# The first expert's weights get a place outside the attention's buffers and are split mostly in the body before the last; sums, sixth tile and last norm stand later

## The chip, the cores and the metric

One core of one Trainium2 chip. The metric is the device time of one launch in microseconds (us); lower is better. The kernel before was timed three times: median 1436.99 us, from 1432.22 to 1437.5.

## The reference, cut to what matters

32 batches of 112 tokens, width 256. First a gated cross-attention over 375 context rows and the 112 normed tokens themselves, 8 heads of 64; then a layer of 8 experts of inner width 1024, of which each token takes the best two.

```python
x = x + tanh(g_xattn) * attention(ctx_1024, layernorm(x), mask, ...)      # softmax over 487 keys
h = layernorm(x)
bids = sigmoid(h @ conf_w.T + conf_b) * wealth                            # 8 bids per token
top_bids, chosen = top_k(bids, 2); weight = softmax(top_bids)
expert(h) = (silu(h @ gate_w.T) * (h @ up_w.T)) @ down_w.T
x = x + tanh(g_ffn) * sum over the chosen of weight * expert(h)
```

## The kernel before, in words

Every matrix product is done in halves: each operand is scaled by a power of two and split into a high and a low f16 part (names ending in `_hi`, made on ACT, and `_lo`, made on DVE), and TensorE (PE) multiplies three of the four pairs.

**Attention.** A loop over the batches, written out as 32 bodies b = 0 to 31 (B = 32, so B - 1 is body 31, the last). Each body has eight slots h, one per head, and every engine has its own program for a slot. In slot h of body b PE computes scores (`sims`, two heads at once in even slots), transposes of the probabilities (`probs_T`), products with the values (`values`), one or two projections for the next batch (`piece`, into the two PSUM tiles `fP`), and what is left of batch b - 1 (`heads_T`, `out_proj`, `norm2_T`). ACT does exponentials (L769), high halves of probabilities (L776) and projections (L762); DVE does the masked maximum (`masked_max`, tile `ms`, L1036), the low halves (L1042, L1026), the residual of batch b - 1 (`residual`, L1067, which frees the store of `x1`) and the routing arithmetic. Each engine takes its own program strictly in order; semaphores tie them.

**Experts.** Tokens are written to `routed_rows` by expert (GpSimd's indirect DMAs, `scatter`), and a second loop runs over NT = 63 tiles of 128 rows: transpose of the tile (`tile_T`), `gate_up` for the two halves i = 0, 1 of the inner width (into `gP`, `uP`), `silu` on ACT, `gated` on DVE, transpose (`act_T`), and `down` into `yP`, weighted by `weigh` and added to `out` by a DMA (`add_tile`). In step t PE takes `act_T(t - 1, 1)`, `tile_T(t + 1)`, `gate_up(t, 0)`, `gate_up(t, 1)`, `down(t - 1)`. Only the first AHEAD = 5 tiles, of the fullest expert, can be read before all tokens are scattered; tile 5, the sixth, is the first that needs every scatter to have landed.

**An expert's weights.** They come as f32 into `raw` in six pieces of 128 x 1024 and are split into `W2`. The stages, by name: `expert_squares` (ACT, L854, sums of squares of a piece), `expert_sums` (PE, L1655, adds them over the partitions), `expert_bound` (DVE, L1245), `expert_pow` (GpSimd, L522), `expert_scale` (DVE, L1251 to L1258), and per piece `expert_hi` (ACT, L864) and `expert_lo` (DVE, L1263). For the first expert to be used, number 0, all this happens during the last attention bodies: which slot gets which piece is written by hand in `SPLIT_SQ`, `SPLIT_HI` and `SPLIT_LO`; which expert it is, is worked out on DVE in the twelve steps of `ORDER_AT` (the last of them writes `first_i`, L1225), and then SyncE loads it (`load_raw(0)`, L394). For later experts p the same is spread over five tiles: squares after tiles with t % 5 = 0, 1, 2, sums, bound and scale at t % 5 = 3, the split at 3, 4 and 0. From p = 2 on `expert_sums(p)` stands between the two halves of `gate_up` and `expert_bound(p)` ahead of `gated(t, 1)`.

**Memory.** The expert loop's buffers share the memory of the attention's. `W2` has five places of 24 KB per partition: four that are used by PE and one in which experts 4 to 7 are split before they go to DRAM (`split_experts`). The attention's buffers reach up to about 136 KB. The first place lies over `kT0`, `v0` and `qT0`, which body 30 still reads; the wait on `s_pv` in `expert_hi` keeps the first split behind that body.

**The end of the attention.** SyncE's program (the queue of its DMAs) after the last body's loads is: store of `x1` of batch 30, which waits for `residual(30)` in slot 7 of body 31; eight writes of padding rows (`routed_rows<-padrows`, L423); the six pieces of expert 1 (`load_raw(1)`); and only then the store of `x1` of batch 31. GpSimd waits for that last store before it goes into the expert loop, whose first steps are the eight scatters of the last four batches (`scatter_last`) among two `add_tile`, and then the load of tile 5 (`load_tile`, tile `xt`).

Of the kernel before, what the change touches and what calls it, by code (L numbers as in the profile page):

```python
# [14 lines left out]
P = 128  # L15
# [67 lines left out]
SPLIT_SQ = {(B - 3, 7): (0,), (B - 2, 1): (1,), (B - 2, 2): (2,), (B - 2, 5): (3,), (B - 2, 6): (4,), (B - 2, 7): (5,)}  # L83
SPLIT_HI = {(B - 1, 4): (0,), (B - 1, 5): (1,), (B - 1, 6): (2,), (B - 1, 7): (3,)}
SPLIT_LO = {(B - 1, 5): (0,), (B - 1, 6): (1,), (B - 1, 7): (2,)}
ORDER_AT = {(B - 4, 0): (0, 1), (B - 4, 6): (2, 3, 4), (B - 4, 7): (5, 6, 7), (B - 3, 0): (8, 9, 10, 11)}
# [4 lines left out]
def build(nc, x, ctxt, mask, scal, lnw, wqkv, wout, confw, confbw, wffn, out):  # L91
# [4 lines left out]
    with ctx:  # L96
# [153 lines left out]
        W2 = sb("W2", [P, SLOTS + 1, 2, WCOL], F16, pb)  # L250
# [4 lines left out]
        ysb = [sb(f"ysb{i}", [P, D], F32, pb) for i in range(2)]  # L255
        ppb = ExitStack()
# [78 lines left out]
        def in_place(p):  # L335

            return min(p, SLOTS)
# [12 lines left out]
        def _(sp):  # L350
# [61 lines left out]
            def load_place(n):  # L412

                step_ = WCOL // RELOADS
                for c in range(RELOADS):
                    sp.dma_start(W2[:, n % SLOTS, :, c * step_:(c + 1) * step_],
                                 wsp[n - SLOTS, :, :, c * step_:(c + 1) * step_]).then_inc(s_there, 16)
# [23 lines left out]
        def _(pool):  # L441
# [82 lines left out]
            def put_pieces(p, some):  # L524
# [3 lines left out]
                pool.dma_start(wsp[p - SLOTS, :, :, cols], W2[:, SLOTS, :, cols]).then_inc(s_wput, 16)  # L528
# [60 lines left out]
            def body(b, g, q):  # L589
# [7 lines left out]
                if holds(b, 0, B - 4):  # L597
                    rstd(b + 3)
                if b == B - 1:
                    expert_pow(0)  # L600
# [99 lines left out]
        def _(act):  # L700
# [155 lines left out]
            def expert_hi(p, c):  # L856

                if c == 0:
                    act.wait_ge(s_esc, p + 1)
                    if p == 0:  # L860
                        act.wait_ge(s_pv, H * (B - 1))
# [49 lines left out]
            def step(t, k):  # L911
# [17 lines left out]
                if t == AHEAD - 1:  # L929
                    tile_hi(t + 1, 1 - q)  # L930
                if t < NT:
                    if 0 not in TURNED:
                        act_hi(t, q, 0)
                    silu(t, 1, place)
                    if 0 in TURNED:
# [8 lines left out]
            def tail():  # L944

                probs_hi(B - 1, H - 2)
                expert_hi(0, 4)
# [3 lines left out]
                expert_hi(0, 5)  # L951
# [15 lines left out]
        def _(dve):  # L967
# [301 lines left out]
            def body(b, g, q):  # L1269
# [4 lines left out]
                for h in range(H):  # L1274
# [48 lines left out]
                    if (b, h) == (B - 1, 2):  # L1323
                        expert_bound(0, fP[0])
                    if (b, h) == (B - 1, 3):
# [97 lines left out]
            def step(t, k, place, last_place):  # L1423
# [13 lines left out]
                if t == AHEAD - 1:  # L1437
                    tile_lo(t + 1, 1 - q)
# [4 lines left out]
                if p < E and j == 3 and p > 1:  # L1443
                    expert_bound(p, bP)
                if t < NT:
                    gated(t, 1, place)
                    if 0 in TURNED:
# [5 lines left out]
                if p < E and j == 3 and p > 1:  # L1453
                    expert_scale(p)
# [18 lines left out]
            def tail():  # L1473
# [3 lines left out]
                expert_lo(0, 3)  # L1477
# [5 lines left out]
                expert_lo(0, 4)  # L1483
# [389 lines left out]
```

## Time and profile before

| | |
|---|---|
| time, median of three | 1436.99 us |
| the profiled execution | 1435.85 us, span 1434.3 us |
| PE busy | 1351.1 us, 94% |
| DVE busy | 1023.5 us, 71% |
| ACT busy | 934.8 us, 65% |
| GpSimd busy | 488.2 us, 34% |
| mean granted clock of PE | 0.989 of full |

The times in the rows further down are microseconds from the start of the span. The attention's bodies take up about the first 850 us, some 25 us each; the expert loop the rest, about 8.6 us a tile.

### The profile page before, as it was taken

Reading aid. Unit: us, or ns where it says so; the run is one execution under the profiler, and the core shown is the slowest. Engines: PE = TensorE matmul, PEld = TensorE weight load, DVE = VectorE, ACT = ScalarE, POOL = GpSimd, SP = SyncE. Lnnn points to the kernel's source line nnn. Section 1 sums busy time; section 2 is a strip of 40 time slices with the busy share of each in tenths; the row PEclk is TensorE's granted clock in tenths of the full one; section 3 lists DMA queues with packets and bytes.
Section 4 is the critical chain, followed back from the end, with each engine's and each line's share of the span. In section 5 each row is a group of like instructions: output and inputs, shape, how many; then the busy total and the mean of one; then the engine's idle time right before and its main releaser. Section 6 shows DMA issues by size and latency. Waiting matters only on the chain.

```text
span 1434.3 us, 41525 instructions
## 1 busy us (share of the span) xinstructions
PE 1351.1 (94%) x13880; PEld 969.2 (68%) x13880; DVE 1023.5 (71%) x2528; ACT 934.8 (65%) x1932; POOL 488.2 (34%) x659
## 2 busy tenths in 40 slices
PE   2999999999999999999999979999999999999996
PEld 1466666666666666666665657688878778887784
DVE  4688888888888888888888776566556654444442
ACT  5687878787787878878787765566656663333331
POOL 4423322433433334334333143433344333222221
PEclk9999999999999999999999979999999999999998
DMA  4010101111111111111112146433376753112461
GB/s 119 27 42 26 42 23 29 52 40 49 34 53 30 41 46 39 49 33 53 31 33 96 41 129 196 107 98 93 98 211 178 228 152 94 31 31 35 120 203 16
DMA packets 56913, 109.26 MB, mean 76 GB/s; under 512 B 10832, under 2 KB 34768, under 8 KB 56720
## 3 DMA queue, kind: packets, MB, share of 16 engines
q0 software_dynamic: 23712, 55.71, 15.2%
q1 hardware_dynamic: 32160, 49.86, 11.2%
q8 instruction: 126, 2.06, 0.6%
q10 hardware_dynamic: 848, 1.07, 0.3%
q14 instruction: 67, 0.55, 0.1%
HBM read 69.16 MB, written 37.45 MB: 74 GB/s over the span
## 4 chain that ended last, share of the span: by engine, by line
PE 70%; DVE 10%; ACT 6%; issue 6%; DMA 5%; SPq 1%; POOL 1%; POOLq 0%; DVEq 0%; ACTq 0%
PE fP L1542 19%; PE yP L1542 10%; PE uP L1542 10%; PE gP L1542 10%; PE simP L1590 5%; PE ptP L1600 4%; PE tP L1542 3%; PE oP L1542 3%; DVE ms L1036 3%; DVE pT L1042 2%; DMA out<-ysb,xt 2%; PE aP L1773 2%; DVE ao L1054 1%; ACT z L732 1%; PE fP L1558 1%
## 5 line engine op out<-in xcount | busy, mean ns | idle before, releaser
L1542 PE MATMUL fP<-zTs,ws 128*128 128x112 f16 (+1 forms) x1536 | 220.3, 294 | 8.7 <-DVE zTs L1378 5.3
L1542 PE MATMUL fP<-ws,zTs 128*128 128x512 f16 x768 | 186.8, 379 | 0.5 <-DVE kT L1026 0.2
L1036 DVE CUSTOM_DVE_ANT_0 ms<-simP,madd,sim_undo 112x488 f32<-112x488 f32 x256 | 183.9, 720 | 3.3 <-PE simP L1590 1.3
L769 ACT ACTIVATE pr<-ms,nmax 112x488 f32<-112x488 f32 x256 | 179.0, 699 | 3.3 <-DVE nmax L1036 0.5
L1042 DVE SCALAR_TENSOR_TENSOR pT<-ptP,pT 122x448 f16<-122x448 f32 x256 | 157.8, 616 | 28.0 <-ACT pT L776 27.3
L1542 PEld LDWEIGHTS fP<-zTs,ws 128*128 128x128 f16 x1536 | 109.8, 99 | 99.7 <-issue 34.9
L1542 PE MATMUL yP<-W,aT 128*128 (+1 forms) x1512 | 175.4, 273 | 1.8 <-DVE aT L1414 1.8
L1542 PEld LDWEIGHTS yP<-W,aT 128*128 128x128 f16 x1512 | 147.6, 98 | 32.8 <-issue 2.5
L1408 DVE SCALAR_TENSOR_TENSOR act_h<-uP,consts,sg 128x512 f32<-128x512 f32 x126 | 94.5, 750 | 103.1 <-ACT sg L899 102.7
L776 ACT ACTIVATE pT<-ptP 122x448 f16<-122x448 f32 x256 | 137.8, 538 | 40.8 <-PE ptP L1600 39.7
L899 ACT ACTIVATE sg<-gP,consts 128x512 f32<-128x512 f32 x126 | 86.5, 686 | 114.6 <-PE uP L1542 114.4
L641 POOL DMA_INDIRECT out<-ysb,xt x63 | 105.2, 1670 | 157.4 <-DVE ysb L1421 143.8
L1542 PE MATMUL oP<-v,pT 122*128 122x64 f16 x3072 | 133.6, 194 | 14.0 <-DVE pT L1042 9.1
L1600 PE MATMUL ptP<-ident,pr 112*122 112x112 f32 x1024 | 142.0, 261 | 0.4 <-DVE filled L1148 0.4
L499 POOL TENSOR_TENSOR zTs<-zT,zTs 128x1200 f16<-128x1200 f32 x31 | 76.5, 2469 | 193.1 <-ACT zTs L750 193.1
L1542 PEld LDWEIGHTS oP<-v,pT 122*128 122x128 f16 x3072 | 121.0, 98 | 26.6 <-DVE pT L1042 26.5
L1600 PEld LDWEIGHTS ptP<-ident,pr 112*122 112x122 f32 x1024 | 114.2, 139 | 25.6 <-issue 0.8
L1542 PEld LDWEIGHTS fP<-ws,zTs 128*128 128x128 f16 x768 | 67.9, 98 | 82.1 <-issue 14.4
L1590 PE MATMUL simP<-kT,qT 64*128 64x488 f16 x768 | 102.7, 372 | 13.3 <-DVE nmax L1036 12.4
L1026 DVE SCALAR_TENSOR_TENSOR kT<-fP,kT 128x488 f16<-128x488 f32 x128 | 84.9, 664 | 37.2 <-ACT kT L762 37.2
L762 ACT ACTIVATE kT<-fP 128x488 f16<-128x488 f32 x128 | 73.8, 576 | 51.4 <-PE fP L1542 51.3
L1026 DVE SCALAR_TENSOR_TENSOR v<-fP,v 122x512 f16<-122x512 f32 x128 | 88.3, 690 | 26.5 <-ACT v L762 26.0
(233 smaller groups left out, 2496.2 us busy)
## 6 DMA issues: line engine op xcount, KB each, us to landing
raw<-wffn POOLq DMA_DIRECT2D x36, 512.0 KB, 6.9
split_experts<-W POOLq DMA_DIRECT2D x12, 1024.0 KB, 10.0
W<-split_experts SPq DMA_DIRECT2D x16, 768.0 KB, 7.9
xc<-ctxt SPq DMA_DIRECT2D x32, 375.0 KB
xt<-routed_rows POOLq DMA_DIRECT2D x63, 129.0 KB, 2.4
raw<-wffn SPq DMA_DIRECT2D x12, 512.0 KB, 9.5
routed_rows<-padrows SPq DMA_DIRECT2D x8, 645.0 KB, 7.9
xl<-x SPq DMA_DIRECT2D x32, 112.0 KB
```

The lines of the kernel that those rows point to most:

```text
L499: nc.gpsimd.tensor_tensor(zTs[p][:, 1, :, :], zT[:, :, :], zTs[p][:, 0, :, :], ALU.subtract).then_inc(s_zsplit, 1)
L641: pool.indirect_dma_start(out[:, :], bass.IndirectOffsetOnAxis(ap=xt[k][:, D:D + 1].bitcast(I32), axis=0), ysb[t % 2][:, :], None, compute ...
L769: nc.scalar.activation(pr[h % 2][:, :], ms[h % 2][:, :], ACT.Exp, bias=nmax[p][:, h:h + 1], scale=-1.0, accum_out=rsum[p][:, h:h + 1]).the ...
L776: nc.scalar.activation(pT[h % 2][:, 0, :, 0:S], ptP[h % 2][0:KR, :, 0:S], ACT.Copy, scale=P_TOP).then_inc(s_pthi, 1)
L899: nc.scalar.activation(sg[i][:, :], gP[i][:, :], ACT.Silu, scale=constant(place, 0)).then_inc(s_silu, 1)
L1026: nc.vector.scalar_tensor_tensor(out=o, in0=i, scalar=1.0 / TOP, in1=hi, op0=ALU.mult, op1=ALU.subtract).then_inc(s_plo, 1)
L1036: nc.vector.tensor_tensor_reduce(out=ms[h % 2][:, :], in0=simP[h % 2][0:S, 0:NK], in1=madd[p][:, :], scale=sim_undo[0:S, 0:1], scalar=3.0e ...
L1042: nc.vector.scalar_tensor_tensor(out=pT[h % 2][:, 1, :, 0:S], in0=ptP[h % 2][0:KR, :, 0:S], scalar=P_TOP, in1=pT[h % 2][:, 0, :, 0:S], op0 ...
L1408: nc.vector.scalar_tensor_tensor(out=act_h[i][:, :], in0=uP[i][:, :], scalar=constant(place, 2), in1=sg[i][:, :], op0=ALU.mult, op1=ALU.mu ...
L1542: last = nc.tensor.matmul(o, lhs(k, a), rhs(k, c), start=n == 0, stop=n == len(todo) - 1)
L1590: last = nc.tensor.matmul(simP[i][:, 0:NK], qT[p][r, a, h // 2, :], kT[p][r, c, h // 2, :], start=t == 0, stop=t == len(PARTS) - 1)
L1600: last = nc.tensor.transpose(ptP[h % 2][0:KR, c, 0:S], pr[h % 2][:, c * KR:(c + 1) * KR], ident[0:S, 0:S])
```

## The change

The order in which `W2` and the buffers around it are laid out changes: `W2` now stands last, and expert 0 uses its fifth place, above all the attention's buffers. The places are renumbered for this (`in_place`, `in_slot`), and the wait on `s_pv` falls away. The twelve ordering steps move up within body 28; the six pieces of squares go from bodies 29 and 30 to 28 and 29; sums, bound, power and scale from body 31 to body 30, with a wait on PE before `fP[0]` is written again; the split of the six pieces from slots 4 to 7 of body 31 and the tail to slots 3 to 7 of body 30 and 0, 1 of body 31. In the expert loop `tile_T(5)` and its halves go behind `gate_up(4, 1)` and `gated(4, 1)`; `expert_sums(p)` for p from 2 goes behind `gate_up(t, 1)`, and `expert_bound(p)` next to `expert_scale(p)` behind `gated(t, 1)`. In PE's tail `norm2_T(31)` goes behind the whole of `gate_up(0, 1)`.

```diff
-SPLIT_SQ = {(B - 3, 7): (0,), (B - 2, 1): (1,), (B - 2, 2): (2,), (B - 2, 5): (3,), (B - 2, 6): (4,), (B - 2, 7): (5,)}
-SPLIT_HI = {(B - 1, 4): (0,), (B - 1, 5): (1,), (B - 1, 6): (2,), (B - 1, 7): (3,)}
-SPLIT_LO = {(B - 1, 5): (0,), (B - 1, 6): (1,), (B - 1, 7): (2,)}
-ORDER_AT = {(B - 4, 0): (0, 1), (B - 4, 6): (2, 3, 4), (B - 4, 7): (5, 6, 7), (B - 3, 0): (8, 9, 10, 11)}
+SPLIT_SQ = {(B - 4, 6): (0,), (B - 4, 7): (1,), (B - 3, 0): (2,), (B - 3, 3): (3,), (B - 3, 5): (4,), (B - 3, 7): (5,)}
+SPLIT_HI = {(B - 2, 3): (0,), (B - 2, 4): (1,), (B - 2, 5): (2,), (B - 2, 6): (3,), (B - 2, 7): (4,), (B - 1, 0): (5,)}
+SPLIT_LO = {(B - 2, 4): (0,), (B - 2, 5): (1,), (B - 2, 6): (2,), (B - 2, 7): (3,), (B - 1, 0): (4,), (B - 1, 1): (5,)}
+ORDER_AT = {(B - 4, 0): (0, 1), (B - 4, 1): (2, 3), (B - 4, 3): (4, 5, 6, 7), (B - 4, 4): (8, 9, 10, 11)}
...
         def in_place(p):
-            return min(p, SLOTS)
+            return (min(p, SLOTS) + SLOTS) % (SLOTS + 1)
+        def in_slot(n):
+            return (n % SLOTS + SLOTS) % (SLOTS + 1)
...
+                if b == B - 2:
+                    expert_pow(0)
                 if b == B - 1:
-                    expert_pow(0)
                     first_rows(0, 2)
...
-                    if p == 0:
-                        act.wait_ge(s_pv, H * (B - 1))
...
-                if t == AHEAD - 1:
-                    tile_hi(t + 1, 1 - q)
                 if t < NT:
...
                     silu(t, 1, place)
+                    if t == AHEAD - 1:
+                        tile_hi(t + 1, 1 - q)
...
-                    if (b, h) == (B - 1, 2):
+                    if (b, h) == (B - 2, 1):
                         expert_bound(0, fP[0])
-                    if (b, h) == (B - 1, 3):
+                    if (b, h) == (B - 2, 3):
                         expert_scale(0)
...
-                if p < E and j == 3 and p > 1:
-                    expert_bound(p, bP)
                 if t < NT:
                     gated(t, 1, place)
+                    if t == AHEAD - 1:
+                        tile_lo(t + 1, 1 - q)
...
                 if p < E and j == 3 and p > 1:
+                    expert_bound(p, bP)
                     expert_scale(p)
...
                     if holds(b, 0, B - 2):
+                        if (b, h) == (B - 2, 2):
+                            pe.wait_ge(s_ech, 1)
...
-                    if (b, h) == (B - 1, 1):
-                        pe.wait_ge(s_plo, seq(B - 2, NPIECE))
+                    if (b, h) == (B - 2, 1):
+                        pe.wait_ge(s_plo, seq(B - 2, PQ + 1) + 1)
                         expert_sums(0, fP[0])
...
-                gate_up(0, 0, 1, 0, (0,))
+                gate_up(0, 0, 1, byte_of(0))
                 norm2_T(B - 1, (B - 1) % 4)
-                gate_up(0, 0, 1, 0, (1,))
...
-                if t == AHEAD - 1:
-                    tile_T(t + 1, (t + 1) % XT_BUFS)
-                if SPAN < t and t // SPAN + 1 < E and t % SPAN == 3:
-                    expert_sums(t // SPAN + 1, bP)
...
                     gate_up(t, q, 1, byte)
+                if t == AHEAD - 1:
+                    tile_T(t + 1, (t + 1) % XT_BUFS)
+                if SPAN < t and t // SPAN + 1 < E and t % SPAN == 3:
+                    expert_sums(t // SPAN + 1, bP)
```

## Rows read from the trace of the kernel before

**Rows 1.** Busy us (x instructions) of PE, PEld, DVE, ACT, POOL, PE's clock, DMA, by stretch.
```profile
773.73:799.40 25.67, 24.39 (x254) 16.18 (x255) 21.09 (x57) 18.69 (x43) 6.23 (x6) 1.00 0.46 157
799.40:824.30 24.90, 23.93 (x247) 15.28 (x247) 19.18 (x50) 20.38 (x48) 4.11 (x6) 1.00 0.07 21
824.30:847.20 22.90, 17.35 (x202) 12.41 (x202) 20.10 (x62) 17.67 (x40) 6.50 (x9) 0.83 0.16 44
...
1200.00:1300.00 100.00, 100.00 (x1062) 81.16 (x1061) 43.24 (x70) 33.08 (x58) 25.94 (x24) 1.00 0.19 35
```
**Rows 2.** Timeline of PE around tile 5: start us, us, instruction, idle before it.
```profile
900.40 0.44 PE L1737 MATMUL xP<-ident,xt 128*128 128x128 f32 x2 [2.85 <-DMA xt<-routed_rows]
900.67 2.38 PE L1542 MATMUL gP<-W,xT 128*128 128x512 f16 x6
...
904.95 2.79 PE L1542 MATMUL yP<-W,aT 128*128 128x256 f16 x24
...
908.22 1.50 PE L1542 MATMUL gP<-xT,W 128*128 128x128 f16 x24
```
**Rows 3.** The chain that ended last, from the last store to tile 5.
```profile
868.72 11.23 DMA out<-x
...
897.91 2.44 DMA xt<-routed_rows
```
**Rows 4.** Timeline of SyncE's DMA queue: expert 0, a store, padding, expert 1.
```profile
779.24 3.28 SPq L394 DMA_DIRECT2D raw<-wffn  x6
...
847.21 0.33 SPq L375 DMA_DIRECT2D out<-x  x1
848.32 12.92 SPq L423 DMA_DIRECT2D routed_rows<-padrows  x8
862.58 6.01 SPq L394 DMA_DIRECT2D raw<-wffn  x6
```
**Rows 5.** Instructions on tile raw, 740 to 825 us: its six loads, from issue.
```profile
DMA to landing us min/median/max: 3.9/6.2/8.5
```
**Rows 6.** Instructions of lines L864, L1263, L854: duration ns min/median/max.
```profile
L864 ACT ACTIVATE W<-raw,escale x48: 1132/1137/1158, 838.2 to 1182.0; 128x1024 f16<-128x1024 f32 x48
L1263 DVE SCALAR_TENSOR_TENSOR W<-raw,escale,W x48: 1273/1276/1285, 840.7 to 1184.7; 128x1024 f16<-128x1024 f32 x48
L854 ACT ACTIVATE junk<-raw x48: 1041/1056/1074, 800.2 to 1159.7; 128x1024 bf16<-128x1024 f32 x48
```
**Rows 7.** Timeline of DVE in body 30, slots 5 and 7.
```profile
818.82 0.62 DVE L1042 SCALAR_TENSOR_TENSOR pT<-ptP,pT 122x448 f16<-122x448 f32 x1 [0.80 <-ACT pT L776]
...
823.43 0.72 DVE L1036 CUSTOM_DVE_ANT_0 ms<-simP,madd,sim_undo 112x488 f32<-112x488 f32 x1
```
**Rows 8.** Timeline of DVE in body 31: scale, the third split, residual of batch 30.
```profile
835.15 0.17 DVE L1251 TENSOR_SCALAR ebits<-epow 128x3 int32<-128x3 int32 x1 [0.18 <-POOL epow L522]
...
836.56 0.73 DVE L1036 CUSTOM_DVE_ANT_0 ms<-simP,madd,sim_undo 112x488 f32<-112x488 f32 x1 [0.21 <-DVE consts L1258]
...
845.46 1.27 DVE L1263 SCALAR_TENSOR_TENSOR W<-raw,escale,W 128x1024 f16<-128x1024 f32 x1
846.65 0.48 DVE L1067 SCALAR_TENSOR_TENSOR x<-tP,gates,xres 112x256 f32<-112x256 f32 x1
```
**Rows 9.** PE's waits from 900 us on: waited for, us in total, times, longest.
```profile
PE bP L1655 <- ACT junk L854: 3.2, 3, 1.4
```
**Rows 10.** Timeline of PE at the tile in which expert 5's sums stand.
```profile
1070.15 0.39 PE L1655 MATMUL bP<-esq,ones 128*128 128x6 f32 x2 [1.08 <-ACT junk L854]
...
1072.98 2.78 PE L1542 MATMUL yP<-W,aT 128*128 x24
...
1081.66 2.78 PE L1542 MATMUL yP<-W,aT 128*128 x24
```
**Rows 11.** Timeline of DVE at the same tile: low half of its activations.
```profile
1079.46 0.69 DVE L1414 TENSOR_TENSOR aT<-aP,aT 128x512 f16<-128x512 f32 x1
```
**Rows 12.** Timeline of PE in the tail: the last norm's transposes.
```profile
863.10 0.41 PE L1629 MATMUL tP<-ident,z 112*128 112x112 f32 x2 [1.98 <-DVE z L1081]
```

More of the change, by code:

```diff
@@ L249, in build @@
         junk = sb("junk", [P, PCOL], BF16, pb)
-        W2 = sb("W2", [P, SLOTS + 1, 2, WCOL], F16, pb)
         xT = [sb(f"xT{i}", [P, 2, KD, P], F16, pb) for i in range(2)]
@@ L255, in build @@
         ysb = [sb(f"ysb{i}", [P, D], F32, pb) for i in range(2)]
+        W2 = sb("W2", [P, SLOTS + 1, 2, WCOL], F16, pb)
         ppb = ExitStack()
@@ L415, in load_place @@
                 for c in range(RELOADS):
-                    sp.dma_start(W2[:, n % SLOTS, :, c * step_:(c + 1) * step_],
+                    sp.dma_start(W2[:, in_slot(n), :, c * step_:(c + 1) * step_],
                                  wsp[n - SLOTS, :, :, c * step_:(c + 1) * step_]).then_inc(s_there, 16)
@@ L527, in put_pieces @@
                 pool.wait_ge(s_wlo, p * PIECES + some[-1] + 1)
-                pool.dma_start(wsp[p - SLOTS, :, :, cols], W2[:, SLOTS, :, cols]).then_inc(s_wput, 16)
+                pool.dma_start(wsp[p - SLOTS, :, :, cols], W2[:, in_place(SLOTS), :, cols]).then_inc(s_wput, 16)
             def next_raw(p, c):
@@ L946, in tail @@
                 probs_hi(B - 1, H - 2)
-                expert_hi(0, 4)
                 tile_hi(0, 0)
@@ L950, in tail @@
                 norm2_out(B - 2)
-                expert_hi(0, 5)
                 heads_out_hi(B - 1)
@@ L1436, in step @@
                     gated(t, 0, place)
-                if t == AHEAD - 1:
-                    tile_lo(t + 1, 1 - q)
                 if t < NT and 0 not in TURNED:
@@ L1476, in tail @@
                 norm2(B - 2, (B - 2) % 4)
-                expert_lo(0, 3)
                 tile_lo(0, 0)
@@ L1482, in tail @@
                 logits(B - 2, (B - 2) % 4)
-                expert_lo(0, 4)
                 heads_out_lo(B - 1)
-                expert_lo(0, 5)
                 tile_lo(1, 1)
@@ L1707, in tail @@
                 pe.wait_ge(s_wlo, 4)
-                gate_up(0, 0, 0, 0, (0,))
+                gate_up(0, 0, 0, byte_of(0), (0,))
                 out_proj(B - 1)
-                gate_up(0, 0, 0, 0, (1,))
-                gate_up(0, 0, 1, 0, (0,))
+                gate_up(0, 0, 0, byte_of(0), (1,))
+                gate_up(0, 0, 1, byte_of(0))
                 norm2_T(B - 1, (B - 1) % 4)
-                gate_up(0, 0, 1, 0, (1,))
                 confidences(B - 1)
@@ L1746, in byte_of @@
             def byte_of(place):
-                return place % SLOTS * (2 * WCOL * 2)
+                return in_slot(place) * (2 * WCOL * 2)
             def gate_up(t, q, i, slot_, some=(0, 1)):
@@ L1801, in step @@
                     gate_up(t, q, 0, byte)
-                if t == AHEAD - 1:
-                    tile_T(t + 1, (t + 1) % XT_BUFS)
-                if SPAN < t and t // SPAN + 1 < E and t % SPAN == 3:
-                    expert_sums(t // SPAN + 1, bP)
                 if t == 1:
@@ L1832, in _ @@
             weights_there(0)
-            byte, last_byte = 0, 0
+            byte = last_byte = byte_of(0)
             for t in range(1, NT + 1):
```

## The prediction

> **What bounds the kernel now.** I read the busy times by stretch first. In the expert loop PE has no free time at all [rows 1], so there only PE's own work and its waits count. In the attention's last three bodies it is otherwise: PE is busy for 24.39 of 25.67 us in body 29 and 23.93 of 24.90 in body 30, but only for 17.35 of 22.90 in body 31, at a mean clock of 0.83, while DVE is busy for 20.10 there [rows 1]. So body 31 is bound by DVE and ACT, in which the splitting of expert 0 stands, and bodies 29 and 30 by PE, with DVE and ACT at three quarters to four fifths.
>
> Then PE's timeline in the first tiles. It stands still for 2.85 us at 900.40 for the rows of tile 5 [rows 2], the longest wait of the expert loop. I followed that wait back through the chain of waits: load of tile 5, scatters, GpSimd's wait for the last store of x1, which took 11.23 us from its issue at 868.72 [rows 3]. In SyncE's queue that store stands behind eight padding writes and six pieces of expert 1, issued from 848.32 to 868.6 without a gap, and these behind the store of batch 30 at 847.21 [rows 4], which waits for DVE's residual(30) at 846.65 [rows 8]. This is the clock of the hand-over: **tile 5 arrives 53 us after residual(30)** (900.40 less 847.2), whatever PE does in between. PE's position ahead of tile 5 is worth nothing as long as it gets there first.
>
> Last, PE's waits in the rest of the loop: three times it waits in expert_sums for ACT's squares, 3.2 us in all [rows 9], for experts 5, 6 and 7.
>
> **Part 1: the sixth tile.** Before, tile_T(5) stood ahead of gate_up(4, 1). From the arrival at 900.40 PE had the transposes, gate_up(4, 1), down(3) at 904.95, act_T and a transpose, and began gate_up(5, 0) at 908.22: 7.82 us [rows 2]. After, gate_up(4, 1) runs in the time of the wait. What is left from the arrival on: transposes 0.27 (900.40 to 900.67), and what ran from 904.95 to 908.22, 3.27; 3.54 us, if the clock is full. It was not: gate_up(4, 1) took 4.28 us from 900.67 to 904.95 [rows 2], where the same half and expert 5's sums take 2.83 at full clock, 1070.15 to 1072.98 [rows 10], so 2.6 without the sums; 1.7 us were lost to the half clock (1.2 in place of 2.4 GHz) that the wait brought. Will PE still wait? It now reaches tile_T(5) 2.6 us later in its own work, but the tail gets shorter for it by about as much or more (part 3), so the wait stays near 2.8 us and I take the 1.7 us as lost again: 3.54 + 1.7 = 5.2, gain 7.8 - 5.2 = **2.6 us**. Other end: with no fall of the clock, 4.3. Not less than 2.6 unless the low halves that follow are late: they are hidden by down(3), 2.6 us (2.79 by its row, the pipeline included). What is late next is expert_scale(1), which waits for GpSimd's power; it sits on DVE, and its splits lie under gate_up(5).
>
> The Trainium skill, "TensorE: Matmul & The Clock Gate", section "HAM oscillation", says that a wait for a DMA puts TensorE back to half rate, and that the loss is half of the throttled time. The rows agree here: 4.28 us for 2.6 of work. By that rule the 1.7 us come back whenever PE still waits at tile 5 as long as before; if the sixth tile's move ends the wait, the gain would be 4.3 and not 2.6.
>
> **Part 2: the split, in what it moves residual(30).** One high half takes 1.14 us on ACT, one low half 1.28 on DVE (1.20 from start to start in a row), one square 1.06 and its read-out some 0.15 [rows 6].
>
> *Bodies 28 and 29.* Order of the loads: expert 0's six pieces were issued at 779.24 to 782.5 and landed 3.9 to 8.5 us after issue [rows 4, 5]; the first square was at 800.2 [rows 6]. The order is now known some five slots of 3.1 us (25 / 8) earlier, and the first square stands two slots behind it, 6 us: enough for a first piece at 1 + 3.9 us, with one us to spare, and each next one comes a slot or more later. No wait charged. ACT gets two squares in body 28 and four in 29: 18.69 + 4 x 1.2 = 23.5 of 25.67 us [rows 1], so there is room, but a square in slot 0 of body 29 stands ahead of zT and kT, which free fP for PE. The twelve ordering steps only change places. I charge **0.5 us** (0, all hidden, to 1.5, one and a half squares exposed).
>
> *Body 30.* ACT: five squares out, five high halves in: even. DVE: bound 0.35, scale 1.4 (835.15 to 836.56 [rows 8]), four low halves 4.8: 19.18 + 6.5 = 25.7 us on DVE in a body of 24.90 [rows 1]. DVE becomes the bound of body 30. If every gap were filled the body would grow by 0.8; if none, by 6.5. Most of its gaps are waits for ACT (0.80 at 818.82 is one [rows 7]). Laid out slot by slot with these durations: slot 3 takes the scale with a net 0, slots 4 and 5 each a low half in the gap behind them, but from residual(29) on nothing is left to fill; the last masked maximum of body 30, at 823.43 [rows 7], slides by 2.5 us and the first of body 31 by **3.5**. GpSimd's power is queued ahead of rstd1(29), which waits longer anyway.
>
> *Body 31.* Low halves 4 and 5 in slots 0 and 1 fall into waits for ACT and PE, 0.4 more. Bound and scale leave: -1.6 by slot 4. Three low halves (and four high ones) leave between 836.56 and 846.65 [rows 8], 3 x 1.2 = 3.6, of which the chain scores, exponential, transpose, out_proj gives back 2.6. Residual(30) then is at +3.5 + 0.4 - 1.6 - 2.6 = -0.3, with body 29 at **+0.2 us, that is 0**. With the ends of body 30 (0.8 and 6.5) and of bodies 28 and 29 it is -3 to +4. So the work is moved out of one DVE-bound body into another that becomes so, and tile 5 arrives when it did.
>
> **Part 3: the tail.** Without low halves 3 to 5 PE comes out of the tail earlier against residual(30), by 2 to 3 us, and norm2_T(31), which made PE wait 1.98 us [rows 12], now stands behind 1.3 us more of gate_up. All this is ahead of tile 5, and PE only waits longer there: **0**. It would count in full (some 4 us) only if tile 5 were no longer waited for.
>
> **Part 4: sums later.** 3.2 us of waits [rows 9] end, because gate_up(t, 1), 2.6 us, covers the longest, 1.4. But expert_bound now stands behind gated(t, 1), and DVE then waits for GpSimd's power (0.9 us) ahead of the scale: some 1.2 us more on DVE ahead of weigh(t - 1), two low halves and act_lo(t, 1), six times. At expert 5 act_lo(t, 1) runs from 1079.46 to 1080.15 and down(t) at 1081.66 [rows 10, 11]. PE earlier by 1.1 asks for it at 1080.6, and DVE, without the 0.35 of the bound ahead of gated but with 1.2 behind, ends at about 1080.7: a wait of 0.1. At expert 6, with 1.4, some 0.3. Gain 3.2 - 0.5 = **2.7 us**. Ends: 3.9, if the stretched matmul ahead of each wait counts as well (0.2 each); 0, if the later scale costs PE half a us in each of six tiles.
>
> **Sum.** 2.6 + 0 + 0 + 2.7 = 5.3 us. The profiled execution had 1435.85 us, so 1430.5; it lies 1.1 us under the median of the three, so against the median it is 1431.7. I say **1431 us**.
>
> **The rivals.**
> A, *the hand-over moves up* (faster by more than 0.5%, 7.2 us, about what a measurement of this kernel can tell from no change). DVE's gaps in body 30 take the low halves, residual(30) comes 3 us earlier, and PE's wait at tile 5 ends with the clock held: 4.3 + 3 + 3 = 10.3, 1426 us. For it: DVE has 5.7 us free in body 30 and needs 6.5 [rows 1]. Against it: its gaps come where it waits for ACT, which is busy for 20.38 of 24.90. Chance 0.33.
> B, *body 30 falls behind* (slower side). Each low half there delays the maximum, that the exponential, that the next low half; nothing is hidden, body 30 grows by 6.5, squares cost 1.5, PE's idle time ahead of the ranks in body 31 puts its clock at half for another 3 us, 1.5 lost. Residual(30) is then 4 + 1.5 late or more, and gains of parts 1 and 4 are eaten from 5.3 on: 1435 to 1440, 1437 for the case. To be slower by over 0.5% it takes 12.5 us. For it: PE's maximum, exponential and transpose form one loop. Chance 0.15, of which 0.05 past the bound.
> C, *the scale is the new wait*. Part 4 gives nothing, as at experts 2 to 7 down(t) waits for act_lo(t, 1): 1435.85 - 2.6 = 1433. Against it: act_lo stands 1.5 us ahead of down at expert 5. Chance 0.12.
> D, *tile 5 isn't set by the last store*, and only PE's own order counts; then the tail counts too: 5.3 + 4, 1427. Against it: GpSimd starts its first scatter right as the store lands. Chance 0.05, and on A's side.
>
> **Chances.** My case has 0.35. Its own range is 1428 to 1434. Faster by over 0.5%: A, D, 0.38 less what of A stays under 7.2 us, 0.04, and 0.02 from the edge of my case: 0.36. Slower: 0.05 from B and 0.04 for a mean of stalls that I have not seen: 0.09. The rest, 0.55, is no difference that can be told. The range for 8 in 10 takes in A at 1425 and most of B at 1437.
>
> **What would show it.** Sums of expert 0 in body 30, and bodies 30 and 31 at about 27.5 and 20 us; store of batch 30 at 847 within 3 us; padding and expert 1 behind it at the same pace; tile 5's transpose at about 900 behind gate_up(4, 1), with a wait of some 2 to 4 us and the clock at half in down(3); no waits for L854 in expert_sums, and short ones of yP for DVE's aT instead. I am wrong if residual(30) moves by more than 3 us either way, or if PE no longer waits at tile 5.

## The result, and the profile after

The changed kernel took 1442.93 us in the median of six runs (1440.84 to 1444.42), the kernel before 1435.49 beside it. The ratio is 1.0045, 95% interval 1.0032 to 1.0059: by it the changed kernel is some 6.5 us slower, where I had forecast 5.3 us faster. The profiled execution had 1444.42 us, span 1442.5.

The stretches that answer to [rows 1] (columns as there), bodies 29, 30 and 31 up to the store of batch 30:

```profile
773.87:801.40 27.53, 24.90 (x255) 16.24 (x255) 20.16 (x50) 23.76 (x55) 6.90 (x7) 1.00 0.30 101
801.40:828.69 27.29, 24.22 (x249) 15.55 (x249) 23.80 (x62) 20.98 (x45) 5.69 (x6) 1.00 0.06 19
828.69:851.86 23.17, 17.79 (x197) 13.14 (x198) 18.68 (x53) 14.36 (x34) 4.79 (x8) 0.78 0.14 37
```

Body 29 is 1.9 us longer, body 30 2.4, and body 31, from which DVE lost 1.4 and ACT 3.3 us of work, is no shorter. Below is the queue of SyncE's DMAs, which answers to [rows 4]:

```profile
851.86 0.33 SPq L379 DMA_DIRECT2D out<-x  x1
852.98 13.88 SPq L427 DMA_DIRECT2D routed_rows<-padrows  x8
868.22 5.78 SPq L398 DMA_DIRECT2D raw<-wffn  x6
874.12 0.45 SPq L379 DMA_DIRECT2D out<-x  x1
```

The store of batch 30 goes out 4.65 us later than before, the last store 5.4 later. PE's timeline around tile 5, which answers to [rows 2], and down(5) at the end of the next tile:

```profile
904.18 1.46 PE L1539 MATMUL gP<-W,xT 128*128 128x512 f16 x6
...
906.77 0.40 PE L1735 MATMUL xP<-ident,xt 128*128 128x128 f32 x2
907.70 2.78 PE L1539 MATMUL yP<-W,aT 128*128 128x256 f16 x24 [0.52 <-DVE aT L1415]
...
910.97 1.50 PE L1539 MATMUL gP<-xT,W 128*128 128x128 f16 x24
...
916.67 0.50 PE L1539 MATMUL yP<-W,aT 128*128 128x256 f16 x3 [0.27 <-DVE aT L1415]
```

The wait for tile 5 is all but gone (what is left of it is 0.3 us of a weight load, L1735) and the clock holds: gate_up(4, 1) takes 2.59 us (904.18 to 906.77) in place of 4.28. The step that holds the move, from one act_T to the next, took 9.28 us in place of 13.33. The start of step 1 (its act_T) was 4.75 us later than before (874.63, was 869.88), that of step 5 2.7 us (910.31, was 907.57), and that of step 62 8.4 (1417.00, was 1408.64). So the loop behind tile 5 lost 5.6 us more, although the waits of [rows 9] are gone. These are the three longest rows of PE's list of waits from 860 us on (in all, times, longest):

```profile
PE yP L1539 <- DVE aT L1415: 2.7, 5, 1.5
PE tP L1626 <- DVE z L1082: 1.0, 1, 1.0
PE uP L1539 <- issue: 0.9, 3, 0.4
```

From 907 to 1420 us all of PE's waits come to 2.4 us, and before to 5.3. So no new wait pays for the 5.6 us: most of them lie in matmuls that got slower. This is tile 10 before (PE, and the gated that its act_T waits for on DVE):

```profile
950.31 0.75 DVE L1408 SCALAR_TENSOR_TENSOR act_h<-uP,consts,sg 128x512 f32<-128x512 f32 x1 [0.33 <-ACT sg L899]
...
952.01 0.60 PE L1773 MATMUL aP<-ident,act_h 128*128 128x128 f32 x4
...
952.66 1.50 PE L1542 MATMUL gP<-xT,W 128*128 128x128 f16 x24
954.00 1.56 PE L1542 MATMUL uP<-xT,W 128*128 128x128 f16 x24
955.46 1.46 PE L1542 MATMUL gP<-W,xT 128*128 x6
```

and after:

```profile
954.41 0.75 DVE L1409 SCALAR_TENSOR_TENSOR act_h<-uP,consts,sg 128x512 f32<-128x512 f32 x1
...
955.44 0.60 PE L1771 MATMUL aP<-ident,act_h 128*128 128x128 f32 x4
...
956.10 1.69 PE L1539 MATMUL gP<-xT,W 128*128 128x128 f16 x24
957.75 1.96 PE L1539 MATMUL uP<-xT,W 128*128 128x128 f16 x24
959.70 1.46 PE L1539 MATMUL gP<-W,xT 128*128 x6
```

The same 48 products of gate_up(10, 0) take 3.60 us, 956.10 to 959.70, in place of 2.80. No wait stands at them, the clock is full. What differs is how late gated(9, 1) ended ahead of the act_T in front of them: 0.28 us (955.16 to 955.44) in place of 0.95. I call this the **lead** below. In the changed kernel gate_up(t, 0) takes 3.4 us or more in tiles 6, 10, 15, 20, 24, 25, 30, 34, 35 and 61, always behind a lead of at most 0.28 us but for the last; before it was so in 6, 20, 32 (leads of 0.24 and less) and 61. In tiles 6, 24 and 30 PE also stood 0.2 to 0.3 us ahead of act_T, in the others before 61 not at all.

The lead doesn't explain all of the 5.6 us. In the two traces the steps 5 to 35 lost 3.1 us and the steps 36 to 61 lost 2.5, and from 36 to 60 every lead is 0.94 or 0.95 as before. Of the 2.5 us 1.5 are spread over the steps 36 to 59, some 0.06 in each (e1_arith says from what), and 1.0 stands in steps 60 and 61, where PE now waits 0.54 us for the last expert's weights (`W<-split_experts`).

Nor does a short lead cost anything in every tile. This is tile 3 before:

```profile
885.52 0.63 PE L1773 MATMUL aP<-ident,act_h 128*128 128x128 f32 x4 [0.62 <-DVE act_h L1408]
...
886.20 1.50 PE L1542 MATMUL gP<-xT,W 128*128 128x128 f16 x24
...
888.88 1.46 PE L1542 MATMUL gP<-W,xT 128*128 128x512 f16 x6
```

PE even waits for gated(2, 1), which ended 0.26 us ahead of act_T, and the 48 products take 2.68 us (886.20 to 888.88). It is so in tiles 2 (leads from 0.65 up) and 3 of every kernel that keeps act_T ahead of gate_up(t, 0), with one exception: tile 3 of the changed kernel, 3.75 us with two stalls of PE in it. What sets the tiles below 5 apart in the kernel is that their expert is number 0, so the address of its weights is a constant of the program; from tile 5 on it is read from a table and stands in a register. No run here swaps the two.

### The profile page after: what moved, and what is told of

Its sections match the earlier page's. It is cut to its first block, busy times and chain, and to the rows that moved or that the text cites. A ratio compares the mean times of both kernels' runs of the same rounds, so it can differ in the third digit from the quotient of the medians.

```text
span 1442.5 us, 41531 instructions
## 1 busy us (share of the span) xinstructions
PE 1360.9 (94%) x13880; PEld 976.4 (68%) x13880; DVE 1022.9 (71%) x2528; ACT 933.5 (65%) x1932; POOL 487.2 (34%) x659
## 4 chain that ended last, share of the span: by engine, by line
PE 71%; DVE 10%; ACT 7%; issue 6%; DMA 4%; POOL 1%; SPq 1%; DVEq 0%; POOLq 0%; ACTq 0%; another core or an unknown queue 0%
PE fP L1539 18%; PE uP L1539 10%; PE gP L1539 10%; PE yP L1539 10%; PE simP L1587 5%; PE ptP L1597 4%; PE oP L1539 3%; PE tP L1539 3%; DVE ms L1037 2%; DVE pT L1043 2%; PE aP L1771 2%; DMA W<-split_experts 1%; DVE ao L1055 1%; ACT z L737 1%; PE fP L1555 1%
```

## The experiments

Each run was timed in five rounds against the kernel before on the same chip; a ratio is to that kernel, with its 95% interval, and 0.1% is 1.4 us.

**e1_arith: the longer place arithmetic alone.**
```diff
-                return place % SLOTS * (2 * WCOL * 2)
+                return (place % SLOTS + SLOTS + 1) % (SLOTS + 1) * (2 * WCOL * 2)
```


> The kernel before with one edit: the line that turns an expert's place into a byte offset takes one addition and one more modulo, as in the changed kernel, with the same value as before. Layout, schedule and order of work stay. Theory P (place arithmetic in TensorE's queue): after the changed kernel's tile 5 the loop lost 5.7 us against before although its sums won 3.3, and 48 products of some gate_up(t, 0) start 75 ns apart in place of 56; if the longer arithmetic is what leaves the queue without a lead, this run is slower than before by 4 to 9 us, with more tiles of some 9.4 us. Theory M (the new layout of the memory slows the products): no change, within 1 us. Theory S (the loop is slow only because the schedule ahead of it differs): no change.

1.0000 (0.9990 to 1.0011). Theory P is out as the main cause: at most 1.6 us. A small part of it stays: the 24 steps 36 to 59, in which nothing is split, took 208.21 us here and 207.91 to 208.29 in the eight traces with this arithmetic (the changed kernel, e1, e2, e4, e8, e9, e15, e16), against 206.80 to 207.24 in the five with the old one and no other edit there (before, e5, e6, e7, e12). That is some 1.1 us, 0.05 a tile, at the same lead of 0.95.

**e2_layout: the new layout alone**, with that arithmetic and without the wait on s_pv.


> The kernel before with only the new layout: W2 last, places renumbered with the longer arithmetic, no wait on s_pv. Schedule of the split, sixth tile, sums and last norm as before. Theory M: slower by 4 to 9 us, all of it in the expert loop, and more than e1_arith. Theory P: the same time as e1_arith within 1 us. Theory S: within 1 us of before.

1.0015 (1.0004 to 1.0027). The expert loop from step 5 to 62 took 501.08 us against 501.07: theory M is out. In the trace the 2 us lie ahead of the loop: 0.4 came by PE's wait for the ranks in body 31, and 1.4 more by residual(30); e7_bound_early has those 1.4 too, with no edit there, so they can be chance (last section). The steps 36 to 59 took 1.1 us more than before, as in e1_arith. What else the ratio's 2.2 us hold has no mechanism here.

**e3_cheap: places counted downwards.**
```diff
-            return (n % SLOTS + SLOTS) % (SLOTS + 1)
+            return SLOTS - n % SLOTS
```


> The changed kernel with the places counted downwards (expert n in place 4 - n % 4, the fifth used in place 0), so that one modulo and one subtraction do where the changed kernel has two modulos and an addition. Expert 0 still lies above the attention's buffers. Theory P: faster than the changed kernel by 2 to 6 us, 1437 to 1441. Theories M and S: 1443, as the changed kernel.

1.0083 (1.0070 to 1.0096), 5.5 us slower than the changed kernel: a miss. It was not cheaper. Its page counts 41647 instructions, the changed kernel's 41531: 116 more, which would be two for each of the 58 tiles whose expert is read from a table (e1_arith counts 41525, as before). In tiles 36 to 53 gate_up(t, 0) takes 2.91 to 3.07 us against 2.72 to 2.88, at the same lead.

**e4_oldsplit: the changed kernel with the old schedule** of orders, squares, sums and split.


> The changed kernel with the split's old schedule: orders, squares, sums, bound, power, scale and the six splits stand where they stood before; layout, longer arithmetic, sixth tile, later sums and last norm are as changed. If the schedule costs what residual(30) and the tail show (4.65 and 3.9 us later), this run is faster than the changed kernel by 3.5 to 5 us, 1438 to 1439.5, with bodies 30 and 31 and residual(30) as before. Rival (the loss all arises in the expert loop, since PE would have waited for tile 5 anyway): 1442 to 1443.

1.0016 (1.0002 to 1.0029). Against the changed kernel's 1.0045 that is 4.2 us: the schedule costs what I expected here, and the rival is out. Residual(30) is back at 846.10, where the kernel before had 846.65.

**e5_sums: part 4 alone.**


> The kernel before with part 4 alone: expert_sums(p) behind gate_up(t, 1) and expert_bound(p) next to expert_scale(p). My forecast of the part: 2.7 us faster than before. Theory L, formed on the traces so far: the later scale pushes ACT's high halves and with them gated(t - 1, 1) to within 0.3 us of the transpose act_T that waits for it (0.95 us otherwise), and the gate_up(t, 0) behind such a late arrival takes 3.5 to 3.6 us in place of 2.8. By L the waits for L854 go (3.2 us) but gate_up(t, 0) of tiles 10, 15, 25, 30, 35 (and one or two more) is 0.8 us longer: between 1 us faster and 3 us slower than before.

1.0020 (1.0007 to 1.0032): 2.9 us slower. The waits of [rows 9] are gone, and gate_up(t, 0) of tiles 10, 15, 25, 29, 30 and 35 took 3.56, 3.46, 3.41, 3.52, 3.72 and 3.63 us, at leads of 0.10 to 0.25: 4.7 us more than before in these six. The profiled execution was the fastest of the twelve (1437.17), and its loop from step 5 to 62 took 501.09 us against 501.07; so this trace shows the gain eaten, and not the 2.9 us on top.

**e6_sixth: part 1 alone.**


> The kernel before with part 1 alone: tile 5's transpose and halves behind gate_up(4, 1). My forecast: 2.6 us faster, 4.3 if the clock stays full. By the changed kernel's trace, in which the fifth step took 9.28 us in place of 13.33, it is 4 us, unless tile 5's rows come later than TensorE; then each us of that wait is lost again. So 3 to 4 us faster, and 1 us of that lost again if act_lo(4, 1) is only just ready for down(4).

0.9990 (0.9976 to 1.0004), 1.4 us faster, less than expected but with 3 us inside the interval. In its trace step 4 takes 9.58 us in place of 13.33, and step 5 0.8 us more (9.38), with a wait of down(4) for act_lo.

**e7_bound_early: the sums later, the bound where it was.**


> The kernel before with only the move of expert_sums(p) behind gate_up(t, 1); expert_bound(p) keeps its place ahead of gated(t, 1). Then GpSimd's power and the scale are not later by more than the sums themselves, and what DVE waits for in expert_bound lies under the silu. Theory L: the waits for the squares go and no gate_up(t, 0) is stretched in exchange: 2 to 3.5 us faster than before, and faster than e5_sums by 2 to 5 us. Rival (gate_up is stretched for another reason than the late gated): the same time as e5_sums.

0.9994 (0.9982 to 1.0006): no change against before, but 3.7 us faster than e5_sums. Tiles 10, 15, 25 and 35 are back at 2.89, 2.77, 2.71 and 2.85 us. Why it still gains nothing is seen at experts 5 to 7: ACT's squares are late as before (they wait for raw), act_lo of the same tile comes 0.14 us ahead of down in place of 1.68, and gate_up of tiles 24, 29 and 34 takes 3.52, 3.19 and 3.68 us. The waits moved.

**e8_after_bound: the same in the changed kernel**
```diff
                 if p < E and j == 3 and p > 1:
-                    expert_bound(p, bP)
                     expert_scale(p)
...
+                if p < E and j == 3 and p > 1:
+                    expert_bound(p, bP)
                 if t < NT:
                     gated(t, 1, place)
```


> The changed kernel with one edit: expert_bound(p) stands ahead of gated(t, 1) again, the sums stay behind gate_up(t, 1). Theory L: the stretched gate_up(t, 0) of tiles 10, 15, 25, 30, 35 go back to 2.8 us, 3 to 5 us faster than the changed kernel, 1438 to 1440. Rival (stretched for another reason, such as the new place of the weights): no change, 1443.

1.0015 (1.0003 to 1.0027), 4.3 us faster than the changed kernel. Theory L holds, the rival is out. Tiles 10, 15 and 35 are back at 2.89, 2.81 and 2.86 us; 25 (3.35, lead 0.35) and 30 (3.21, lead 0.68) only in part.

**e9_squares: the changed kernel with only orders and squares early.**


> The changed kernel with only the orders and squares early (in bodies 28 and 29); sums, bound, power, scale and the split stand where they stood before. It stands between e4_oldsplit (both old) and the changed kernel (both new), which are 4.2 us apart. From the changed trace: body 29 is 1.9 us longer than before, body 30 2.4 and residual(30) 4.65 later. If the squares in bodies 28 and 29 are what makes body 29 longer, this run is about 1.9 us slower than e4_oldsplit, 1441, with body 30 starting at 801.4 and as long as before (24.9); the rest, 2.4, is the low halves in body 30. Rival: all 4.2 us come from body 30, then 1439.

1.0032 (1.0020 to 1.0045), 2.3 us slower than e4_oldsplit. Body 30 started at 801.3 and was 24.6 us long. So of the schedule's 4.2 us, 2.3 are the squares and 1.9 the rest, each give or take some 1.8.

**e10_late: DVE late on purpose, PE never waiting.**
```diff
+                late = 0 if i == 0 else 256 if 38 <= t < 45 else 512 if 47 <= t < 54 else 0
+                if late:
+                    nc.vector.scalar_tensor_tensor(out=junk[:, 0:late], in0=uP[i][:, 0:late], ...)
                 nc.vector.scalar_tensor_tensor(out=act_h[i][:, :], in0=uP[i][:, :], ...
```


> The kernel before with work added on DVE alone, in tiles without any split: ahead of gated(t, 1) the same operation once more into a scratch buffer, 256 columns wide (some 0.4 us) in tiles 38 to 44 and 512 wide (some 0.7 us) in tiles 47 to 53. The output stays the reference's. TensorE never has to wait for DVE there: act_T follows the end of gated 0.95 us later, so both leave it 0.2 us and more. Plain reading of the waits (what doesn't end a wait costs nothing): same time as before. Theory L: gate_up(t + 1, 0) is longer by 0.3 to 0.5 us in seven tiles and by 0.7 to 0.8 in the other seven, 7 to 9 us slower than before, about 1444.

1.0055 (1.0038 to 1.0072): 7.9 us slower. This is DVE and PE in one tile of the first group:

```profile
1217.45 0.48 DVE L1410 SCALAR_TENSOR_TENSOR junk<-uP,consts,sg 128x256 bf16<-128x256 f32 x1 [0.29 <-ACT sg L899]
1217.85 0.74 DVE L1412 SCALAR_TENSOR_TENSOR act_h<-uP,consts,sg 128x512 f32<-128x512 f32 x1
```
```profile
1228.83 1.50 PE L1546 MATMUL gP<-xT,W 128*128 128x128 f16 x24
1230.17 1.90 PE L1546 MATMUL uP<-xT,W 128*128 128x128 f16 x24
1232.03 1.46 PE L1546 MATMUL gP<-W,xT 128*128 x6
```

The second fence is the following tile: the first 24 products run at 56 ns (1.34 / 24), the next 24 at 78 (1.86 / 24). The seven tiles behind the small dose (lead 0.56 in place of 0.95) were 0.40 us longer each, the seven behind the large one (0.29) 0.66 each: 7.4 us in all. No wait of PE stands in the trace from 1195 to 1360 us. The added operation can't slow the products by running beside them, since it ends ahead of act_T. So for the tiles from 5 on theory L is shown by intervention; why a short lead costs is not.

**e11_turn: the kernel before with act_T(t - 1, 1) behind gate_up(t, 0)**, ACT and DVE in the same order.
```diff
-                act_T(t - 1, 1)
...
                 if 1 < t < NT:
                     gate_up(t, q, 0, byte)
+                    act_T(t - 1, 1)
```


> The kernel before with act_T(t - 1, 1) behind gate_up(t, 0) in each tile, and ACT and DVE in the same order; every product as before. The wait for gated(t - 1, 1), which stood right ahead of the short products of gate_up(t, 0), is then long fulfilled when TensorE comes to it. Theory L: gate_up(t, 0) takes its shortest time, 2.68 us, in all tiles: 0.1 us won in some 55 tiles and 0.8 in three or four, 5 to 9 us faster than before, unless down(t - 1) now waits for act_lo (0.8 us of slack by the rows), which would cost 0.3 us a tile, and 10 us slower in the worst case. Rival (gate_up is stretched by its own reads of the weights): no gain, or slower.

0.9973 (0.9961 to 0.9986): 3.9 us faster. Two tiles in a row:

```profile
1090.82 0.38 PE L1743 MATMUL xP<-ident,xt 128*128 128x128 f32 x2
1091.04 1.50 PE L1548 MATMUL gP<-xT,W 128*128 128x128 f16 x24
1092.38 1.50 PE L1548 MATMUL uP<-xT,W 128*128 128x128 f16 x24
1093.72 0.61 PE L1779 MATMUL aP<-ident,act_h 128*128 128x128 f32 x4
...
1099.37 0.38 PE L1743 MATMUL xP<-ident,xt 128*128 128x128 f32 x2
```

In all but six of the tiles 5 to 61 the 48 products take 2.67 to 2.69 us, and most tiles are 8.55 us long. The exceptions are tiles 7, 10, 20, 32, 35 and 61, with 2.82, 2.71, 3.17, 3.50, 2.75 and 3.90 us. The gain is under 5 to 9 us because step 31 (10.70) waits 1.16 us for DVE's act_lo ahead of down, which also stretches tile 32, and because PE waits in step 60 (11.12) for the last expert's weights on their way back from DRAM:

```profile
1395.61 0.44 PE L1743 MATMUL xP<-ident,xt 128*128 128x128 f32 x2 [1.14 <-DMA W<-split_experts]
1395.88 1.95 PE L1548 MATMUL gP<-xT,W 128*128 128x128 f16 x24
```

**e12_best: parts 1, 3's last norm and the later sums, with the bound early**, on the kernel before.


> The kernel before with the sixth tile's move, the last norm's move and the later sums with the bound kept ahead of gated(t, 1); layout and schedule of the split as before. Measured singly: -1.2 us for the sixth tile, 0 for the sums with the early bound. If these add: 1 to 3 us faster than before, 1433 to 1435. Rival (the last norm's move brings something by itself, which no run has shown alone): 3 to 4 us faster.

0.9975 (0.9956 to 0.9994), 3.6 us faster. The interval doesn't tell the forecast from the rival.

**e13_both: e11_turn and e12_best together.**


> e12_best and e11_turn together: the kernel before with the sixth tile and last norm later, sums later with the bound early, and act_T(t - 1, 1) behind gate_up(t, 0). Singly they are 0.25% and 0.27% faster than before. If they add in full: 7.5 us, 1428. By theory L they add in part only: e12_best still has some seven stretched gate_up (tiles 20, 24, 29, 30, 32, 34, 61), which e11_turn removes too, but e11_turn has two waits of some 1 us for DVE's act_lo at tiles 28 and 31: 5 to 8 us, 1427 to 1431.

0.9947 (0.9931 to 0.9964): 7.6 us faster than before, the best of all. Singly they gave 3.9 and 3.6: they add, as far as the intervals tell.

**e14_after_turn: the changed kernel, turned.**


> The changed kernel with the same order as e11_turn. If the part of its loss that lies in the expert loop is all the lead of TensorE's queue ahead of gate_up(t, 0), the turned loop takes every step in 8.55 us whatever DVE's lateness, and this run comes out at e11_turn plus what the schedule costs (4.2 us) less what the sixth tile brings (1 to 3): 1433 to 1436, 7 to 10 us faster than the changed kernel. Rival (part 4 costs by something else too): 1437 or more.

1.0007 (0.9994 to 1.0019), 5.5 us faster than the changed kernel, less than expected, and the rival is partly right: steps 9, 19, 24, 29 and 34 still take 9.2 to 9.6 us, because with the late scale act_lo is only 0.13 to 0.27 us ahead of down.

**e15_spaced: the squares later and in other slots.**
```diff
+SPLIT_SQ = {(B - 3, 3): (0,), (B - 3, 4): (1,), (B - 3, 5): (2,), (B - 3, 6): (3,), (B - 3, 7): (4,), (B - 2, 0): (5,)}
```


> The changed kernel with the six squares in slots 3 to 7 of body 29 and slot 0 of body 30 in place of slots 6 and 7 of body 28 and 0, 3, 5, 7 of body 29. In the changed trace three squares run on ACT between 773.5 and 779.9, where ACT has no gap, and zT is 2.5 us later; body 29 is 1.9 us longer. If it is where they stand that costs: body 29 grows by less than 1 us and this run is 1 to 2 us faster than the changed kernel. Rival (ACT's sum over body 29 decides): the same 1443, or slower, since five squares stand in body 29 in place of four.

1.0029 (1.0020 to 1.0037), 2.3 us faster than the changed kernel. Bodies 29, 30 and 31:

```profile
773.90:799.10 25.20, 24.49 (x256) 16.06 (x257) 20.28 (x50) 22.35 (x52) 6.86 (x7) 1.00 0.31 109
799.10:827.30 28.20, 24.39 (x250) 15.58 (x252) 23.87 (x62) 22.03 (x48) 5.71 (x6) 1.00 0.06 18
827.30:850.12 22.82, 19.72 (x184) 14.82 (x184) 18.34 (x51) 14.01 (x33) 4.29 (x6) 0.63 0.12 30
```

Body 29 with five squares is shorter than with four. The place decides, not the sum; body 30 took 0.9 us of it back.

**e16_low31: all six low halves in body 31.**
```diff
+SPLIT_LO = {(B - 1, 0): (0,), (B - 1, 1): (1,), (B - 1, 2): (2,), (B - 1, 3): (3,), (B - 1, 4): (4,), (B - 1, 5): (5,)}
```


> The changed kernel with all six low halves in slots 0 to 5 of body 31; high halves, scale and squares as changed. My forecast was that low halves only move between one DVE-bound body and another: then body 30 is back at some 25 us, body 31 longer by as much, and the time is that of the changed kernel within 1.5 us. Rival 1 (low halves are dearer in body 30, since each delays the loop of maximum and exponential): 1 to 3 us faster than the changed kernel. Rival 2 (body 31, which the last chain runs through, is the worse place): 1 to 3 us slower.

1.0020 (1.0009 to 1.0032), 3.6 us faster than the changed kernel: rival 1. Bodies 30 and 31:

```profile
801.40:826.30 24.90, 24.14 (x250) 15.52 (x252) 20.46 (x59) 20.39 (x44) 4.83 (x6) 1.00 0.07 20
826.30:848.20 21.90, 17.09 (x182) 12.32 (x183) 21.52 (x55) 14.28 (x34) 5.22 (x8) 0.77 0.12 31
```

Body 30 is back at 24.90, and residual(30) is at 848.20, 21.90 us from body 31's start, with DVE busy in 21.52 of them. In the changed kernel it took 22.6 us with only 18.68 of DVE's work. The six low halves cost nothing in body 31, though they leave no room for more.

**e17_mended: the changed kernel with all four remedies.**


> The changed kernel with all four remedies at once: act_T behind gate_up(t, 0) (singly 0.38% faster than the changed kernel), expert_bound ahead of gated(t, 1) (0.30%, which overlaps with the first), squares in slots 3 to 7 of body 29 and 0 of body 30 (0.16%), low halves in slots 0 to 5 of body 31 (0.25%). If they add but for that overlap: ratio to before 0.995 to 0.997, 1431 to 1434, no better than e13_both (0.9947), which keeps the old layout and the old schedule of the split. Rival (with the other faults mended the earlier split does bring something): under 0.993, faster than e13_both by over 2 us.

0.9957 (0.9940 to 0.9974), inside the forecast and no better than e13_both. The earlier split and the fifth place have no gain of their own that the faults hid, as far as the intervals tell.

## Why the prediction was wrong, step by step

**What bounds the kernel.** The hand-over was read rightly in the main: tile 5's load was issued 52.5 us behind the store of batch 30 (904.35 less 851.86), 50.7 before. (The 53 us of the forecast run from that store at 847.21, not from residual(30), and between padding and expert 1 the queue had a gap of 1.3 us.) That body 31 is bound by DVE was the wrong reading of [rows 1]. Busy for 20.10 of 22.90 us is no bound: e16_low31 put 1.4 us more into it, with 3.4 less on ACT, and it became shorter.

**Part 1.** 4.05 us in the trace for 2.6 (or 4.3 with the clock held) in the forecast. The step that failed is "the wait stays near 2.8 us", one of my two signs of being wrong: PE began its tail 3.9 us later and not earlier, lost 2.1 more in step 3, and came to tile 5 only 0.3 us ahead of its rows. The clock held since the wait ended, as the rule that I cited from the Trainium skill, "TensorE: Matmul & The Clock Gate", section "HAM oscillation", has it. Next on the path were waits for act_lo, 0.52 and 0.27 us, and a tile 0.86 us longer. Alone the part brought 1.4 us (e6_sixth, from 3.4 faster to 0.6 slower).

**Part 2** was forecast at 0 and cost 4.2 us (e4_oldsplit). *Bodies 28 and 29*: charged at 0.5 us (0 to 1.5), the trace has 1.9 and e9_squares against e4_oldsplit 2.3. I summed ACT's busy time, although I had named the danger, a square ahead of zT. This is ACT of the changed kernel there:

```profile
773.50 1.05 ACT L859 ACTIVATE junk<-raw 128x1024 bf16<-128x1024 f32 x1
...
776.36 1.06 ACT L859 ACTIVATE junk<-raw 128x1024 bf16<-128x1024 f32 x1
...
778.98 1.07 ACT L859 ACTIVATE junk<-raw 128x1024 bf16<-128x1024 f32 x1
...
780.02 1.24 ACT L749 ACTIVATE zT<-fP,lnv 128x375 f32<-128x375 f32 x2
...
808.07 0.58 ACT L767 ACTIVATE kT<-fP 128x488 f16<-128x488 f32 x1 [1.49 <-PE fP L1539]
```

Three squares within 6.5 us and no gap between, zT at 780.02 where it was at 777.50. ACT's free time (1.49 us at 808.07) lay elsewhere. *Body 30*: the last masked maximum moved from 823.43 [rows 7] to 827.82, 2.4 us more than the body's start did: the 2.5 of the forecast. *Body 31*: there the step failed that gives back 1.6 us for bound and scale and 2.6 for the halves. Up to the maximum at 836.56 [rows 8], now at 842.70, the body lost 1.75 us where I had it win 1.2: low half 4 stood ahead of the ranks' operand (L1141), PE waited 2.21 us for it in place of 1.01, and its mean clock over the body was 0.78 in place of 0.83. From that maximum to residual(30) it won 1.5 us and not 2.6. So nothing came back in all: residual(30) was at 851.30, +4.65 in place of +0.2, with 2.0 brought in from body 29 and 2.4 from body 30. DVE, freed of the halves, stood waiting at the end:

```profile
848.11 0.62 DVE L1043 SCALAR_TENSOR_TENSOR pT<-ptP,pT 122x448 f16<-122x448 f32 x1
850.76 0.62 DVE L1043 SCALAR_TENSOR_TENSOR pT<-ptP,pT 122x448 f16<-122x448 f32 x1 [2.03 <-ACT pT L781]
851.30 0.47 DVE L1068 SCALAR_TENSOR_TENSOR x<-tP,gates,xres 112x256 f32<-112x256 f32 x1
```

So the halves went from a body in which they cost nothing (e16_low31) to one in which each stands in the loop of maximum and exponential. This is rival B, priced at 1437 with part 4's gain in it.

**Part 3.** Rightly 0 in the sum. PE came out 0.7 us earlier against residual(30), not 2 to 3 (gate_up(1, 0) at 870.32, +3.9). The last norm's move was never run alone.

**Part 4** holds the largest error: 2.7 us faster in the forecast, 2.9 slower alone, 5.6 us apart. The waits went, 3.2 us as said. The 0.5 us charged against them was the wrong price: the ratio asks for a cost of some 6, and the trace of e5_sums shows 4.7. I looked only at whether DVE would be late enough for PE to wait. It was late by less than that, and the 0.8 us of gate_up behind it, in six tiles, stands in no list of waits. Rival C, that part 4 gives nothing because down waits for act_lo, had the sign of the trouble but not its place: such waits behind tile 5 came to 1.2 us, before to 1.8.

**The sum from single runs**: part 1 -1.4, part 4 +2.9, layout +2.2, schedule +4.2: 7.9 us against 6.5 measured, each with about 1.8 to either side. The layout, charged at nothing, is the term with only half a cause: the longer arithmetic that comes with it costs some 1.1 us in the steps 36 to 59, and the rest is open. I had looked only at the wait that it takes away. Open too are why a short lead costs nothing in tiles 2 and 3, and the three stalls of PE at 893 to 897 us (the 0.9 us of "issue" above), in a step 2.1 us longer than before.

## What to carry to other kernels

A producer that ends just ahead of its consumer isn't always free: in this loop the short products behind the wait got slower without any wait in the trace, in the tiles whose weights are addressed through a register. Compare the start-to-start time of equal groups of instructions, and put long work, not short, behind the wait that is met last; moving one transpose brought 3.9 us here. That isn't a full cure: a late act_lo ahead of down still stretched the short products behind down (tile 32 of e11_turn). Work is not hidden by an engine's free share of a body, only by a gap at the place where its queue puts it. And a wait that is taken away from one engine is looked for next behind the same late producer.

## What the runs showed of the hardware

**The lead.** Groups of 48 products of 128 x 128, at a full clock, in tiles from 5 on: 2.68 us when act_T stands behind them, 2.7 to 3.1 with a lead of 0.95 us (tile 61 apart), 3.0 to 3.2 with 0.56, 3.3 to 3.6 with 0.29, 3.3 to 3.8 with 0.10 to 0.28. In tiles 2 and 3 they take 2.68 us even with 0.66 and 0.26. Groups of six products of 512 columns behind them kept 1.29 or 1.30 us from start to start in all but single tiles of the loop. That TensorE's queue of decoded work runs empty is my reading, and that it does so only where addresses are worked out from registers would fit tiles 2 and 3. The Trainium skill, "Perfetto Trace Analysis", section "Sequencer Loop", has engine instructions pushed into a queue ahead of the engine, which fits; no run here shows the queue itself.

**The clock's fall is not at a fixed place.** In body 31 the kernel before and e7_bound_early run the same instructions. Before:

```profile
828.22 0.58 PE L1600 MATMUL ptP<-ident,pr 112*122 112x112 f32 x4
828.64 0.51 PE L1542 MATMUL oP<-v,pT 122*128 122x64 f16 x12
```

and e7_bound_early:

```profile
828.45 0.98 PE L1600 MATMUL ptP<-ident,pr 112*122 112x112 f32 x4
829.23 0.84 PE L1542 MATMUL oP<-v,pT 122*128 122x64 f16 x12
```

In the second the clock (mean 0.89 from 824.40 to 829.20, 0.50 from there to 835.00) was at its lower level, 1.2 GHz, one group earlier behind a wait of the same 1.01 us, and the scores of heads 2 and 3 began 1.1 us later. So one profiled execution doesn't place this hand-over sharply: in the nine traces whose program is the same up to there (before, e1, e5, e6, e7, e10, e11, e12, e13) residual(30) stands between 846.12 and 848.55, and in the four with the changed kernel's attention (it, e3, e8, e14) between 850.08 and 851.30. The medians, 846.65 and 850.67, are 4.0 us apart.
